# Second attention: the keep factor inside VectorE's product, a one-row product on TensorE, and shorter leads

## The reference, cut to what matters

```python
def _L1_xattn_ref(queries, keys, values, attention_mask):
    d_keys = jnp.sqrt(jnp.float32(keys.shape[-1]))
    logits = jnp.einsum('bqd,bkd->bqk', queries, keys) / d_keys
    logits = jnp.where(attention_mask < -1.0, attention_mask, logits)
    attn = jax.nn.softmax(logits, axis=-1)
    return jnp.einsum('bqk,bkv->bqv', attn, values)
...
x = x + jnp.tanh(g_ffn[0]) * _L0_ffn_ref(_layernorm(x, axis=-1), ...)
x = x + jnp.tanh(g_xattn[1]) * _L1_xattn_ref(_layernorm(x, axis=-1), ctx_1024, ctx_1024, mask_BxSxS2_fk0)
```

## Time and profile before

| | us |
|---|---|
| median of three runs | 3418.73 (3412.79 to 3420.31) |
| the profiled execution | 3416.94 |
| its span, first to last instruction | 3415.2 |
| the second attention, first load to last residual | about 726.7 to 900.4 |
| mean granted TensorE clock over the span | 0.944 of full |

### The profile page before, as it was taken

One profiled execution on the slowest core, in us unless ns is written; L12 is line 12 of the kernel. 1 busy time (PEld: TensorE's weight loads), 2 busy tenths in 40 slices (PEclk: granted clock), 3 DMA queues, 4 the chain that ended last, 5 costly groups with the idle time before them and its releaser, 6 DMA issues. The chain is left out here.

```text
span 3415.2 us, 61453 instructions
## 1 busy us (share of the span) xinstructions
PE 3084.2 (90%) x23644; PEld 2342.9 (69%) x23644; DVE 2043.6 (60%) x4457; ACT 1416.3 (41%) x2744; POOL 695.9 (20%) x934
## 2 busy tenths in 40 slices
PE   8986699957789999999999999599999997786999
PEld 6864366635579999999999998366676665454543
DVE  3445111128447788788788776366666665586554
ACT  3421111104335555555555555266666665232000
POOL 3443100028200013013012100411111110185000
PEclk9987899979989999999999999699999998797899
DMA  7661111128700000000000000100000000164000
GB/s 235 195 239 47 51 50 50 50 80 252 259 3 1 2 1 2 2 1 2 1 1 2 2 1 1 48 20 20 20 20 19 20 17 7 33 214 137 12 14 19
DMA packets 75488, 183.40 MB, mean 54 GB/s; under 512 B 12215, under 2 KB 18960, under 8 KB 74866
## 3 DMA queue, kind: packets, MB, share of 16 engines
q1 hardware_dynamic: 56452, 135.91, 12.4%
q10 hardware_dynamic: 12606, 29.06, 2.8%
q0 software_dynamic: 6144, 14.50, 1.5%
HBM read 151.83 MB, written 27.79 MB: 53 GB/s over the span
## 5 line engine op out<-in xcount | busy, mean ns | idle before, releaser
L2331 DVE CUSTOM_DVE_ANT_0 probs<-ps,add 112x375 f32<-112x375 f32 x512 | 250.2, 546 | 58.2 <-PE ps L2459 54.4
L2387 ACT ACTIVATE probs<-probs,neg_top 112x375 f32<-112x375 f32 x512 | 282.8, 602 | 4.0 <-DVE neg_top L2331 3.2
L1882 DVE TENSOR_REDUCE top<-ps 112x16 f32<-112x1792 f32 x96 | 194.4, 2025 | 59.6 <-PE ps L2098 58.1
L3033 PE MATMUL ps<-we,xn_t 128*112 128x512 f32 x512 | 227.7, 607 | 1.1 <-DVE x_sb L2953 1.1
L1235 DVE TENSOR_TENSOR hidden<-gated,ps 128x512 f32<-128x512 f32 x64 | 44.0, 688 | 302.7 <-PE ps L1278 302.7
L2484 PE MATMUL ps<-ident,probs 112*125 112x112 f32 x1536 | 222.5, 281 | 2.8 <-DVE probs_t L2338 2.8
L2338 DVE COPY probs_t<-ps 125x336 f32<-125x336 f32 x256 | 129.1, 504 | 151.6 <-PE ps L2484 151.6
L2484 PEld LDWEIGHTS ps<-ident,probs 112*125 112x125 f32 x1536 | 189.7, 188 | 30.7 <-issue 23.0
L1898 DVE TENSOR_TENSOR probs<-probs,inv_sum 112x1792 f32<-112x1792 f32 x96 | 194.4, 2025 | 3.3
L1886 DVE TENSOR_TENSOR probs<-ps,top 112x1792 f32<-112x1792 f32 x96 | 194.4, 2025 | 3.3
L1894 DVE TENSOR_REDUCE row_sum<-probs 112x16 f32<-112x1792 f32 x96 | 193.9, 2020 | 3.2 <-ACT probs L1984 3.2
(11 more groups left out here) (401 smaller groups left out, 6434.1 us busy)
## 6 DMA issues: line engine op xcount, KB each, us to landing
ctx_t<-in_ctx_T_dram SPq DMA_DIRECT2D x128, 375.0 KB, 3.4
ctx_sb<-in_ctx_dram ACTq DMA_DIRECT2D x72, 384.0 KB, 4.4
ctx_sb<-in_ctx_dram SPq DMA_DIRECT2D x32, 384.0 KB
queue<-zeros SPq DMA_DIRECT2D x32, 256.0 KB, 4.8
rows<-queue SPq DMA_DIRECT2D x16, 512.0 KB, 4.1
outputs<-out SPq DMA_DIRECT2D x16, 512.0 KB
mask_in<-in_mask_BxSxS_fk_dram SPq DMA_DIRECT2D x16, 328.1 KB
mask_in<-in_mask_BxSxS_ik_dram SPq DMA_DIRECT2D x16, 328.1 KB
```

The source lines that it names most:

```text
L1882: dve.tensor_reduce(top[:, :, :], scores, AX.X, ALU.max).then_inc(s["top_done"], 1)
L2331: dve.tensor_tensor_reduce(out=probs[:, u, h, :], in0=k.ps[0:S, SCORE + h, 0:L], in1=add[:, j % 2, :], scale=1.0, scalar=BIG, op0=ALU.add, ...
L2387: act.activation(probs[:, u, h, :], probs[:, u, h, :], ACT.Exp, bias=neg_top[:, u, h:h + 1], scale=-1.0).then_inc(s["probs_done"], 1)
L3033: mm = pe.matmul(k.ps[0:S, Y + at % YB, :], xn_t[:, j + u, c, :], we[:, c, e:e + TWO, :].rearrange("p e d -> p (e d)"), start=c == 0, stop ...
```

## The change

1. GpSimd's `keep_mask` goes, with its buffer and semaphore. `kept` is now (`add` == 0) * scores, by the same kind of VectorE instruction, with `add` as first input and the scores in PSUM as second. It waits for `add` (ScalarE) where it waited for `keep` (GpSimd).
2. The minus one comes from TensorE: a product of a row of ones with a row of -1 (1 x 112 by 1 x 375) opens each accumulation of scores, and the two products follow. GpSimd fills the row once with a memset. The wait for the context load now stands behind that product.
3. Leads: `norm(j + 2)` instead of `norm(j + 4)` in VectorE's iteration j, `add_fetched` and `statistics` of j + 5 instead of j + 9, `fetch` of j + 8 instead of j + 12. `rstd` comes in groups of two (after two of one). Ahead of the loop stand four batches of statistics, not nine, and the norms of batches 0 and 1, not 0 to 3. The rings keep their sizes.

```diff
     CT, MR, LAG, XR, FR = 4, 3, 3, 4, 5
-    ADD_LEAD, FETCH_LEAD = 9, 12
-    GROUPS = ((0, 1), (1, 4)) + tuple((j, j + 4) for j in range(4, B, 4))
+    ADD_LEAD, FETCH_LEAD = 5, 8
+    GROUPS = ((0, 1), (1, 2)) + tuple((j, j + 2) for j in range(2, B, 2))
...
-        keep = sb(nc, "keep", [S, 2, L], F32)
+        minus_row = sb(nc, "minus_row", [1, L], F32)
...
             @block.gpsimd
-                def keep_mask(j):
-                    u = j % 2
-                    pool.wait_ge(mask_loaded[j // 2 % MR], 16 * (j // 2 // MR + 1))
-                    if j >= 2:
-                        pool.wait_ge(s["kept_done"], j - 1)
-                    pool.tensor_scalar(keep[:, u, :], mask_in[:, j // 2 % MR, u, :], -1.0, None, ALU.is_ge).then_inc(s["keep_done"], 1)
-
+                pool.memset(minus_row[:, :], -1.0).then_inc(s["row_ready"], 1)
                 fetch(0)
                 fetch(1)
                 norm_scale(0)
                 fetch(2)
+                norm_scale(1)
                 fetch(3)
-                keep_mask(0)
-                norm_scale(1)
-                for j in range(4, 8):
-                    fetch(j)
+                fetch(4)
                 norm_scale(2)
-                for j in range(8, FETCH_LEAD):
+                for j in range(5, FETCH_LEAD):
                     fetch(j)
                 for j in range(B):
-                    if j + 1 < B:
-                        keep_mask(j + 1)
-                    if j % 4 == 3 and j + 5 < B:
-                        norm_scale(group_of[j + 5])
+                    if j % 2 == 1 and j + 3 < B:
+                        norm_scale(group_of[j + 3])
                     if j + FETCH_LEAD < B:
                         fetch(j + FETCH_LEAD)
...
             @block.vector
                     dve.wait_ge(s["scores_done"], j + 1)
-                    dve.wait_ge(s["keep_done"], j + 1)
+                    dve.wait_ge(s["add_done"], j + 1)
                     if j >= 2:
                         dve.wait_ge(s["logits_done"], j - 1)
-                    dve.scalar_tensor_tensor(kept[:, u, :], k.ps[0:S, SCORE + u, 0:L], -1.0, keep[:, u, :], ALU.add, ALU.mult).then_inc(s["kept_done"], 1)
+                    dve.scalar_tensor_tensor(kept[:, u, :], add[:, u, :], 0.0, k.ps[0:S, SCORE + u, 0:L], ALU.is_equal, ALU.mult).then_inc(s["kept_done"], 1)
                     dve.wait_ge(s["kept_done"], j + 1)
-                    dve.wait_ge(s["add_done"], j + 1)
...
-                    if j + XR < B:
-                        norm(j + XR)
-                    if j + ADD_LEAD < B:
-                        add_fetched(j + ADD_LEAD)
-                        statistics(j + ADD_LEAD)
+                    if j + 2 < B:
+                        norm(j + 2)
+                    for i in range(4 if j == 0 else j + ADD_LEAD, min(j + ADD_LEAD + 1, B)):
+                        add_fetched(i)
+                        statistics(i)
...
             @block.tensor
                 def scores(j):
                     u = j % 2
                     pe.wait_ge(s["xn_t_copied"], j + 1)
+                    if j >= 2:
+                        pe.wait_ge(s["kept_done"], j - 1)
+                    if j == 0:
+                        pe.wait_ge(s["row_ready"], 1)
+                    pe.matmul(k.ps[0:S, SCORE + u, 0:L], k.ones[0:1, 0:S], minus_row[:, :], start=True, stop=False)
                     pe.wait_ge(ctx_t_loaded[j % CT], 16 * (j // CT + 1))
-                    if j >= 2:
-                        pe.wait_ge(s["kept_done"], j - 1)
                     for c in range(DC):
-                        mm = pe.matmul(k.ps[0:S, SCORE + u, 0:L], xn_t[:, u, c, :], ctx_t[:, j % CT, c, :], start=c == 0, stop=c == DC - 1)
+                        mm = pe.matmul(k.ps[0:S, SCORE + u, 0:L], xn_t[:, u, c, :], ctx_t[:, j % CT, c, :], start=False, stop=c == DC - 1)
                     mm.then_inc(s["scores_done"], 1)
```

More of the change, by code:

```diff
@@ L1317, in gathered_attention @@
         XNT, SCORE, PT, OUT = 0, 2, 4, 6
-        names = ("one_ready added stats_done mean_done eps_added rstd_done normed xn_transposed xn_t_copied scores_done keep_done add_done "
+        names = ("one_ready added stats_done mean_done eps_added rstd_done normed xn_transposed xn_t_copied scores_done row_ready add_done "
                  "kept_done logits_done probs_done probs_transposed probs_t_copied att_done sum_cut gain_done residual_done")
@@ L1330, in load_masks @@
                     if q >= MR:
-                        sp.wait_ge(s["keep_done"], 2 * (q - MR + 1))
                         sp.wait_ge(s["add_done"], 2 * (q - MR + 1))
@@ L1454, in _ @@
                     statistics(j)
[L1455 to L1461, removed]
+                    if 1 <= j <= 2:
+                        norm(j - 1)
                 for j in range(B + LAG + 1):
@@ L1532, in scores @@
                     pe.wait_ge(s["xn_t_copied"], j + 1)
-                    pe.wait_ge(ctx_t_loaded[j % CT], 16 * (j // CT + 1))
                     if j >= 2:
                         pe.wait_ge(s["kept_done"], j - 1)
+                    if j == 0:
+                        pe.wait_ge(s["row_ready"], 1)
+                    pe.matmul(k.ps[0:S, SCORE + u, 0:L], k.ones[0:1, 0:S], minus_row[:, :], start=True, stop=False)
+                    pe.wait_ge(ctx_t_loaded[j % CT], 16 * (j // CT + 1))
                     for c in range(DC):
-                        mm = pe.matmul(k.ps[0:S, SCORE + u, 0:L], xn_t[:, u, c, :], ctx_t[:, j % CT, c, :], start=c == 0, stop=c == DC - 1)
+                        mm = pe.matmul(k.ps[0:S, SCORE + u, 0:L], xn_t[:, u, c, :], ctx_t[:, j % CT, c, :], start=False, stop=c == DC - 1)
                     mm.then_inc(s["scores_done"], 1)
```

## The result

| | us |
|---|---|
| before, median of four runs | 3419.52 (3412.79 to 3421.25) |
| changed, median of four runs | 3447.72 (3443.68 to 3451.94) |
| ratio changed / before | 1.0088 (95% interval 1.0075 to 1.0100) |
| ratio in a second set of runs of both | 1.0094 (1.0078 to 1.0111) |
| span of the profiled execution, before / changed | 3415.2 / 3442.0 |

The change costs 28.2 us by the medians. The direction and the chain that sets the period were right. The size was not: 3447.7 lies 9.7 us above the forecast of 3438 and 1.7 us above the end of the range. Two terms of the sum failed, the price of the one-row product and the clock, which the sum had at full speed throughout.

A forecast was written before the change was run, and what follows sets the result against it. Bound before: latency in the start, VectorE and GpSimd in the middle, TensorE at the end; then a 5.26 us chain. 20 us won at the start, some 41 lost in 31 periods: 3416.94 + 20.4 = 3437.3, put at 3438; range 3425 to 3446.

The forecast's parts named there:

- The closed chain through `norm(j + 2)`: Middle of the stage: scores, `kept`, sum, gain, residual, norm, transposes, one-row product, scores again; 5.26 us a batch.
- The start: Stage start: it shrinks, with the first `kept` at 751, 20 us earlier, the second at 757, the third at 762.5.
- if TensorE's clock has risen: Stage start: condition for the third `kept` at 762.5, one chain after the second; before the change it had by 756.12.
- The one-row product: TensorE, in the chain ahead of the scores: 0.85 us a batch, between 0.64 by its columns and 0.91.
- The row of the ternary layer: Trace of another one-row product, 512 columns in 1.14 us, which gave the upper end of 0.91 us for 375 columns.
- The clock: TensorE in the middle: clock expected at 1.00, so the chain was summed at full clock.
- The rival of a falling clock: TensorE's clock falls to its lower level in the new gaps: 8.2 us a batch, some 80 us over forecast; chance 2%.
- The sum: Whole stage: 762.5 + 147.3 + 3.9 puts the last `kept` at 913.7, against 893.26 before, 20.4 us later.
- with a period from 4.85 to 5.5: Middle of the stage: the batch periods in us behind the range of 3425 to 3446.
- The first (engines as the bound, 4.12 us): Middle: lead of two suffices, TensorE sets 4.12 us a batch, last `kept` at 878.7, time 3402; chance 8%.
- The second (a product that costs next to nothing): Chain: one-row product nearly free, period 4.41, time 3413, the same as before; chance 6% with other ways there.
- The keep factor at nothing on VectorE: VectorE's `kept`: new form keeps kind and size, 0.55 us; its wait moves to ScalarE's `add`; costed at nothing.

## Why the prediction was right and where it was wrong

**The bound and the chain: right, and shown.** The closed chain through `norm(j + 2)` was worked out as 5.26 us, of which 4.41 without the product. The kernel without the product has a period of 4.41 to 4.48. Making the lead one batch longer, and nothing else, takes the chain away.

**The start: nearly right.** First `kept` at 749.72 (751 forecast, 770.91 before), second at 756.20 (757), third at 763.31 (762.5). The stage begins 1.2 us earlier in this execution (first load at 725.42 against 726.67), so the first `kept` came exactly as forecast behind it, and the third 2 us late. For the third the forecast had set a condition, "if TensorE's clock has risen". It had not: the scores ahead of it still took 2.84 us.

**The one-row product: the first step that failed, a term too small.** "I take 0.85, near this upper end" of 0.91. It measured 0.99, beyond both ends. The row of the ternary layer was the right one to trust over its columns, but from it I read the loss behind the product only, in the place where a product of 256 columns follows; in the chain 0.10 us more also pass ahead of the product and 0.09 in the scores. In 28 periods of 5.40 instead of 5.26 that is 151.2 against 147.3 us: 3.9 us.

**The clock: the second step that failed, a term put at nothing.** The sum had full clock in all 28 periods. The rival of a falling clock was given 2% and a price of 80 us, as if the clock fell for good or not at all. It fell for part of a batch, some seven times: from the third `kept` to that of batch 30 pass 155.4 us, 4.2 more than 28 x 5.40. The argument against it was that TensorE had been idle for 1.2 us with the clock at 1.00 in the earlier trace rows. This compared the idle time and not what stood beside it; the runs show a gap of 0.92 us without a fall where all products have 112 to 128 rows, and with falls where one of 1 or 32 rows is added.

**The sum.** 0.8 + 3.9 + 4.2, and 0.1 in the last period (3.99 against 3.93), are the 9.0 us by which the last `kept` (922.67) is later than the 913.7 forecast. The spans differ by 26.8 us and not by the 29.4 of the last `kept`: behind the last `kept` the changed kernel's execution is 2.6 us shorter, where nothing was changed. That puts the profiled execution 6.4 us above its forecast of 3437.3. The median lies 4.0 us above the profiled execution, where the forecast had 1.8. (3437.3 and 1.8 are 3439.1, not the 3438 that was written down.) With either the product or the clock alone the time would have stayed within the range; with both together it does not. The bound "with a period from 4.85 to 5.5" left no room for a mean of 5.55.

**The rivals.** The first (engines as the bound, 4.12 us) is what the kernel with norm lead three does, at 4.26: the lead of the norm is what kept the changed kernel from it. The second (a product that costs next to nothing) is what the product does in the gap ahead of the transposes.

**The keep factor at nothing on VectorE: right.** The new form takes 0.55 us as the old one did, and its wait for `add` is not the last to end in the changed kernel. With TensorE's product gone `add` sometimes comes as late as the scores, with the same wait of 0.69 us: no row shows it to cost anything.

## What to carry to other kernels

When engines work through batches in a fixed order, write down for every lead which instruction of the other engine it stands behind, and sum the closed chain; with a lead that is too short by one, the chain is the bound while no engine is full, and no busy share shows it. A lead that only fills the start can be shortened where nothing waits for it in the loop (here the statistics and the gathers), and must not take the others with it (here the norm). Work added to a chain should go where its engine waits anyway: the same product cost 0.99 us a batch behind the wait and no more than 0.01 us ahead of it.

## What the runs showed of the hardware

- A float32 product of 112 x 375 over 128 rows costs 0.63 us a batch, in the chain (5.04 against 4.41) and in flow (3.90 against 3.27); over one row it costs 0.99 in both places (5.40 and 4.26), over 32 rows as much in the chain. No weight load runs under the product of few rows, and its own does not run ahead of it. Filling the array with rows of -1/128 instead of one row of -1 made the kernel some 0.5% faster (1.0042 against 1.0088, each against its own runs of the kernel before).
- TensorE's clock fell for parts of batches when an idle gap of 0.92 us a batch met a product of 1 or 32 rows of 0.81 us. It stayed at 1.00 with the same gap beside a product of 128 rows or none, and with the one-row product and a gap of 0.19 us. In one period without a fall, just before one with it, TensorE was busy for 4.48 of 5.40 us; in the kernel with 128 rows, whose clock did not fall, for 32.65 of 40.
- The DMA engines moved 304 GB/s at a shown share of 1.00 (29 us) without becoming the bound, where the kernel before showed 280 at 0.97. At 3.65 us a batch they showed 1.03 and 299 GB/s (60 us), and soon after it the first scores waited for a load, by up to 1.24 us.
- The trace can show a product of TensorE as done before the engines that wait for it go on: in the run with the old leads by 2.5 us (scores recorded to 778.01, waited for until 780.47 and 780.48).
